# Latent attention in a four-layer kernel: score banks per head, a bank of its own for shared products, values in the first and third of four steps

## The chip, the cores and the metric

The kernel runs on one core of a Trainium2 chip. The metric is the device time of one execution in microseconds (us); lower is better. The engines are PE (TensorE; PEld is its weight load), DVE (VectorE), ACT (ScalarE), POOL (GpSimd) and SP (SyncE, which issues DMAs here).

## What is computed

The program runs a stack of layers on 2048 tokens of width 256: an expert layer, gated linear attention, the expert layer again, a dense expert layer, latent attention, and the dense expert layer again. Only latent attention is touched. Its reference, on a normalised input of 4 batches of 512 tokens with a residual added outside:

```python
q = (x @ W_q).reshape(B, S, 16, 128).transpose(0, 2, 1, 3)
latent = x @ W_kv_down                       # 64 wide
kv = (latent @ W_kv_up).reshape(B, S, 16, 128).transpose(0, 2, 1, 3)
scores = jnp.einsum('bhqd,bhkd->bhqk', q, kv) / sqrt(128)
probs = jax.nn.softmax(scores, axis=-1)
out = jnp.einsum('bhqk,bhkd->bhqd', probs, kv)
out = out.transpose(0, 2, 1, 3).reshape(B, S, 16 * 128)
return out @ W_o
```

The weights W_kv_up are folded into the queries (`absorb`) and into the output (`mix`) earlier in the program, so that every head works on the 64-wide latent.

## The kernel before

`latent_attention` works in steps. A step `s` is one tile of 128 query rows of one pair of heads; four steps (`TB`) make a pair, eight pairs (`PAIRS`) a batch, four batches the stage: 128 steps (`NS`) and 32 pairs (`NP`). The engines run their own programs over `s` and meet by semaphores. The order of the work is written out by hand in small tables.

One step goes through these parts, each named by the function that issues it:

- PE `scores(s)`: for each of two heads a product with the high and one with the low part of the latent (L2141, L2142), 128x512 each. Both heads go into one PSUM tile of two banks, `ps_s[s % 2]`, and `s_ready` counts once per step. It waits until the exponentials of step s-2 are done.
- DVE `row_max(s)` (L2381): one reduction over both heads, 1024 elements, gives the negated row maxima.
- ACT `exps(s)` (L2258): two exponentials, one per head, each with its row sum. Both wait for the one reduction.
- DVE `inverse(s)` (L2377): reciprocal of the two sums, when both exponentials are done.
- POOL (L2323): two products scale the probabilities, one per head.
- DVE `probs_turned` (L2388): a 32x32 block transposition of both heads' probabilities. It comes `TLAG` = 2 steps late, between `row_max` and `inverse`.
- PE `values(pair, half)` (L2159): the product of transposed probabilities and latent rows, in two halves of 64 blocks with 128 small matmuls, in two of four steps. It comes `VLAG` = 7 steps late, so that its halves fall on steps with s % 4 = 3 and s % 4 = 0. The result is in `ps_v`, four banks.
- ACT `oT_copy(pair)` (L2263): takes the values out of `ps_v`.

Beside these steps there are shared products, called `miscellany` in the code: queries of a later pair (L2120), a quarter or half of the output of the batch before (`mixed`, L2127), transpositions of the normalised input (L2095), the latent as columns (L2103) and as rows (L2110). They go into the first two banks of `ps_v`, in turn (`bank_of`), in the steps with s % 4 = 1 or 2 (`misc_at`); what stands where is said by `Q_AT`, `MIX_AT`, `TR_AT`, `LATT_AT`, `LATK_AT`. As the banks belong to the values too, `values(pair, 0)` waits until the last two shared products have been taken out of them:

```python
last = last_use(TB * pair + VLAG)
for n in (last - 1, last):
    evicted(pe, uses[n])
```

A product of queries is taken out by ACT in three copies, `q_high` (L2247 twice, L2251): the high parts of both heads, then the whole. POOL `q_low` (L2313, two operations back to back) makes the low parts. `RING` = 3 pairs of queries are kept. DVE's share beside the steps is the statistics and the normalisation of the next batch (L2337, L2341, L2347) and the evictions (L2353, L2361, L2370). SP spreads the latent rows over partitions with 16 DMAs per batch (L2303), which the first values of the batch wait for.

The whole PSUM, eight banks, is used: four by `ps_s`, four by `ps_v`.

## Time and profile before

| | |
|---|---|
| median of 3 runs | 1821.0 us (1817.26 to 1830.79) |
| the profiled execution | 1814.0 us, span 1812.3 us |
| PE busy | 82% of the span |
| DVE, ACT, POOL busy | 60%, 40%, 43% |
| latent attention, first score product to last step's | 1165.0 to 1647.1 us |

All durations are of the profiled execution, whose time is 1814.0 us. A matmul's row shows the time until its result is out, so that matmuls overlap; what PE needs for a piece of work is read from start to start.

### The profile page before, as it was taken

To read this page: it belongs to the slowest core of one execution; us is meant where nothing else is said; L and a number is where in the kernel's file an instruction comes from. 1 tells how busy PE (TensorE), PEld (TensorE's weight loads), DVE (VectorE), ACT (ScalarE), POOL (GpSimd) and SP (SyncE) were. 2 spreads that over 40 slices of the span, in tenths; PEclk is the share of its full clock that TensorE was granted. 3 is DMA by queue.
4 is the path that set the end of the run, shared out by engine and by line. 5 is a ranking of instruction groups with operands and counts; after the bars stand their busy time and mean duration, and the time that the engine had idled before them with its cause. 6 is when DMAs were issued, how large, how long until landed. Compare 5 with 4: busy or idle time off the path is not lost. (4 is left out here: it accounts for less than half of the span.)

```text
span 1812.3 us, 39345 instructions
## 1 busy us (share of the span) xinstructions
PE 1487.1 (82%) x14334; PEld 1022.4 (56%) x14334; DVE 1089.0 (60%) x2639; ACT 732.3 (40%) x1754; POOL 775.6 (43%) x741
## 2 busy tenths in 40 slices
PE   6888995758898978889993778778898887888798
PEld 3555563425555544555662656456576665666576
DVE  6852222476776547832224888576777676664788
ACT  5533332355555425533332111355545545443211
POOL 4453333753300004543336553286766766764000
PEclk9999998679999988899996888888999999989899
DMA  8319995321100005239972221000000000000000
GB/s 248 92 46 262 283 282 170 107 67 53 36 1 1 1 22 161 59 121 279 293 217 85 77 75 52 12 2 3 14 3 2 14 3 3 14 3 3 9 17 21
DMA packets 92662, 145.49 MB, mean 80 GB/s; under 512 B 25032, under 2 KB 52528, under 8 KB 92512
## 3 DMA queue, kind: packets, MB, share of 16 engines
q1 hardware_dynamic: 62816, 93.06, 17.8%
q0 software_dynamic: 15360, 37.77, 6.9%
q10 hardware_dynamic: 14336, 12.59, 2.5%
q8 instruction: 103, 1.69, 0.4%
q14 instruction: 47, 0.39, 0.1%
HBM read 122.39 MB, written 18.87 MB: 78 GB/s over the span
## 5 line engine op out<-in xcount | busy, mean ns | idle before, releaser
L2323 POOL TENSOR_TENSOR sb_m_prob<-sb_m_prob,sb_m_rinv 128x512 f32<-128x512 f32 x256 | 261.4, 1043 | 144.2 <-DVE sb_m_rinv L2377 141.8
L2258 ACT ACTIVATE sb_m_prob<-m_ps_s,sb_m_nmax 128x512 f32<-128x512 f32 x256 | 173.8, 684 | 231.8 <-DVE sb_m_nmax L2381 231.8
L1264 POOL DMA_INDIRECT sb_c_rows<-slot_rows,sb_slot x192 | 192.3, 1001 | 109.1 <-issue 52.0
L2159 PE MATMUL m_ps_v<-sb_m_pT,sb_m_lat_rows 32*64 32x128 f32 x8192 | 161.4, 301 | 61.5 <-ACT sb_m_q_whole L2251 36.2
L2381 DVE TENSOR_REDUCE sb_m_nmax<-m_ps_s 128x2 f32<-128x1024 f32 x128 | 155.8, 1217 | 90.4 <-PE m_ps_s L2142 89.6
L1098 POOL DMA_INDIRECT e_xn<-xn_rows,sb_table x128 | 118.3, 925 | 208.6 <-PE e_ps_x L1176 196.2
L1247 DVE TENSOR_TENSOR sb_e_h<-sb_e_sg,e_ps_gu 96x176 f32<-96x176 f32 x128 | 42.6, 333 | 255.6 <-ACT sb_e_sg L1223 255.6
L2159 PEld LDWEIGHTS m_ps_v<-sb_m_pT,sb_m_lat_rows 32*64 32x64 f32 x8192 | 140.7, 146 | 92.2 <-issue 82.2
L1185 PE MATMUL e_ps_gu<-e_wgu,sb_e_xT 128*96 128x352 f32 x512 | 176.4, 467 | 19.8 <-ACT sb_e_xT L1217 19.2
L2388 DVE STREAM_TRANSPOSE sb_m_pT<-sb_m_prob 128x1024 f32<-128x1024 f32 x128 | 158.0, 1234 | 1.0 <-POOL sb_m_prob L2323 1.0
L2141 PE MATMUL m_ps_s<-sb_m_latT_high,sb_m_qa 128*128 128x512 f32 x256 | 130.7, 511 | 16.5 <-ACT sb_m_prob L2258 13.7
L1202 PE MATMUL e_ps_y<-e_wdn,sb_e_hT 96*96 96x256 f32 x512 | 132.0, 381 | 0.0
L1278 DVE SCALAR_TENSOR_TENSOR sb_x<-sb_c_rows,sb_weight,sb_x 128x256 f32<-128x256 f32 (+1 forms) x192 | 92.5, 482 | 41.8 <-DMA sb_c_rows<-slot_rows,sb_slot 38.4
L1185 PEld LDWEIGHTS e_ps_gu<-e_wgu,sb_e_xT 128*96 128x96 f32 x512 | 73.6, 163 | 60.5 <-ACT sb_e_xT L1217 18.4
L702 PE MATMUL s_ps<-sb_r_xnT,sb_sguT 128*128 128x512 f32 (+1 forms) x192 | 102.2, 682 | 6.5 <-ACT sb_s_up L800 6.5
L2142 PE MATMUL m_ps_s<-sb_m_latT_low,sb_m_qa 128*128 128x512 f32 x256 | 106.4, 416 | 0.0
L293 PE MATMUL d_ps_e<-sb_d_we_high,sb_d_xT_high 128*128 128x512 f32 x256 | 98.7, 468 | 7.3 <-DVE sb_d_xT_low L414 7.3
L2313 POOL TENSOR_TENSOR sb_m_qa<-sb_m_q_whole,sb_m_qa 64x512 fp32r<-64x512 f32 x64 | 81.2, 1268 | 52.9 <-ACT sb_m_q_whole L2251 48.1
L1229 ACT ACTIVATE sb_e_y<-e_ps_y 96x256 f32<-96x256 f32 x128 | 48.7, 380 | 125.0 <-DMA slot_rows<-sb_e_y 91.5
L1775 POOL TENSOR_TENSOR sb_g_gw<-sb_g_g,sb_g_sig 128x512 f32<-128x512 f32 x8 | 11.6, 1448 | 201.2 <-ACT sb_g_sig L1687 201.2
L293 PE MATMUL d_ps_e<-sb_d_we_low,sb_d_xT_high 128*128 128x512 f32 x256 | 85.3, 416 | 0.0
L1217 ACT ACTIVATE sb_e_xT<-e_ps_x 128x192 f32<-128x192 f32 x128 | 42.1, 331 | 105.4 <-ACT sb_e_y L1229 50.2
(278 smaller groups left out, 3103.0 us busy)
## 6 DMA issues: line engine op xcount, KB each, us to landing
e_wgu<-wgu SPq DMA_DIRECT2D x128, 352.0 KB, 4.8
e_wdn<-wdn SPq DMA_DIRECT2D x128, 192.0 KB, 4.6
slot_rows<-sb_e_y ACTq DMA_DIRECT2D x128, 96.0 KB
xn_rows<-e_xn SPq DMA_DIRECT2D x16, 256.0 KB, 2.2
sb_c_rows<-slot_rows,sb_slot POOLq DMA_INDIRECT x192, 2.8
sb_x<-x SPq DMA_DIRECT2D x4, 512.0 KB, 5.6
e_xn<-xn_rows,sb_table POOLq DMA_INDIRECT x128, 5.0
sb_g_zm<-wqT SPq DMA_DIRECT2D x1, 2048.0 KB, 8.8
```

The costliest lines, as they stand in the source:

```text
L293: ins = pe.matmul(ps_e[j][:, :, :], xTs[u][xpart][:, c, :], we[wpart][:, c, 2 * j:2 * j + 2, :], start=(m == 0), stop=(m == 3 * DC - 1))
L1098: pool.indirect_dma_start(x, None, k.xn_rows[:, :], bass.IndirectOffsetOnAxis(ap=k.table[:, e:e + 1], axis=0))\
L1185: ins = pe.matmul(ps_gu[v][:, :], xT[v][:, c, :], wgu[(u - 1) % U][:, c, :], start=(c == 0), stop=(c == DC - 1))
L1202: ins = pe.matmul(ps_y[v][:, :], hT[v][:, c, :], wdn[(u - 3) % U][:, c, :], start=(c == 0), stop=(c == 1))
L1264: pool.indirect_dma_start(rows[u][j][:, :], None, k.slot_rows[:, :], bass.IndirectOffsetOnAxis(ap=k.slot[:, n, j:j + 1], axis=0))\
L2141: pe.matmul(to[:, hh, :], q[:, hh, cols], latT[b % 2][0][:, :], start=True, stop=False)
L2142: ins = pe.matmul(to[:, hh, :], q[:, hh, cols], latT[b % 2][1][:, :], start=False, stop=True)
L2159: ins = pe.matmul(ps_v[rows_of(hh), a, 0:P], lat_rows[b % 2][rows, kb // TB, kb % TB, :], of[rows, hh, :, kb, :], start=(kb == 0), stop=(k ...
L2258: act.activation(prob[s % 4][:, hh, :], ps_s[s % 2][:, hh, :], ACT.Exp, bias=nmax[s % 2][:, hh:hh + 1], accum_out=rsum[s % 2][:, hh:hh + 1 ...
L2323: pool.tensor_tensor(part, part, rinv[s % 2][:, hh:hh + 1].to_broadcast([P, T]), ALU.mult)\
L2381: dve.tensor_reduce(nmax[s % 2][:, :], ps_s[s % 2][:, :, :], AX, ALU.max, negate=True).then_inc(nmax_ready, 1)
L2388: dve.transpose(pT[pair % 2][:, :, t, :, :].rearrange("p h b i -> p h (b i)"), prob[s % 4][:, :, :]).then_inc(turned, 1)
```

## The change

Four things change, all of them in `latent_attention`; the arithmetic is the same.

- The scores have three banks, taken by head: product `j = 2 * s + hh` goes into `ps_s[j % 3]`, `s_ready` counts per head, `row_max` is two reductions of 512 elements, and each exponential waits for its own. `scores` waits head by head for the exponential three products back.
- The shared products have a bank for themselves, `bank`, used by one at a time; the values have `ps_v` alone, and their wait for evictions is gone. `mixed` fills 256 columns of it with one tile of 128 rows and is taken out at once, in the last batch partly by way of `ps_v`.
- The values come 8 steps late, their halves in steps with s % 4 = 0 and 2; queries in steps with s % 4 = 1, always of the pair after next; nearly all other shared products in steps with s % 4 = 3. The transposition of the probabilities is 3 steps late.
- ACT takes the whole query tile out of PSUM first, which frees the bank, and makes the high parts from that copy in SBUF. POOL's two low parts stand in two different steps.

```diff
-    TLAG, VLAG = 2, 7
+    TLAG, VLAG = 3, 8
-    Q_AT = {1: 2, 2: 3, 3: 4, 6: 5, 7: 6, 12: 7, 13: PAIRS, 15: PAIRS + 1}
-    MIX_AT = {4: (0, 0), 5: (0, 1), 8: (1, 0), 9: (1, 1)}
-    TR_AT = {10: 0, 11: 1}
-    LATT_AT, LATK_AT = 14, 0
+    TR_AT, MIX_AT = {18: 0, 22: 1}, {11: 0, 15: 1, 19: 2, 23: 3}
+    LATK_AT, LATT_AT = 3, 27
...
+        if e % TB == 1 and s // TB + 2 < NP:
+            return ("q", s // TB + 2)
...
-        ps_s = [ctx.enter_context(nc.psum_tensor(f"m_ps_s{u}", [P, 2, T], F32)) for u in range(2)]
+        ps_s = [ps(f"m_ps_s{u}", [P, T]) for u in range(3)]
         ps_v = ctx.enter_context(nc.psum_tensor("m_ps_v", [P, TB, T], F32))
+        bank = ps("m_bank", [P, 512])
...
             def take(key):
-                if use_at[key] >= 2:
-                    pe.wait_ge(bank_free[use_at[key] % 2], use_at[key] // 2)
-                return bank_of(key)
+                if use_at[key]:
+                    pe.wait_ge(bank_free, use_at[key])
...
-                if s >= 2:
-                    pe.wait_ge(p_ready, 2 * (s - 1))
                 cols = slice(t * P, (t + 1) * P)
                 for hh in range(2):
-                    pe.matmul(to[:, hh, :], q[:, hh, cols], latT[b % 2][0][:, :], start=True, stop=False)
-                    ins = pe.matmul(to[:, hh, :], q[:, hh, cols], latT[b % 2][1][:, :], start=False, stop=True)
-                ins.then_inc(s_ready, 1)
+                    j = 2 * s + hh
+                    if j >= 3:
+                        pe.wait_ge(p_ready, j - 2)
+                    pe.matmul(ps_s[j % 3][:, :], q[:, hh, cols], latT[b % 2][0][:, :], start=True, stop=False)
+                    pe.matmul(ps_s[j % 3][:, :], q[:, hh, cols], latT[b % 2][1][:, :], start=False, stop=True).then_inc(s_ready, 1)
...
-                    last = last_use(TB * pair + VLAG)
-                    for n in (last - 1, last):
-                        evicted(pe, uses[n])
...
-            for s in range(NS + VLAG - 2):
+            for s in range(NS + VLAG - 1):
                 if s < NS:
                     scores(s)
-                if s >= VLAG and (s - VLAG) % TB < 2:
-                    values((s - VLAG) // TB, (s - VLAG) % TB)
-                if misc_at(s) is not None:
-                    miscellany(misc_at(s))
+                if s >= VLAG and (s - VLAG) % TB in (0, 2):
+                    values((s - VLAG) // TB, (s - VLAG) % TB // 2)
+                if misc_of(s) is not None:
+                    miscellany(misc_of(s))
...
             def q_high(pair):
+                full(("q", pair))
                 if pair >= 2:
                     act.wait_ge(q_ready, 2 * (pair - 1))
-                act.activation(q_whole[pair % 2][:, :], bank_of(key), ACT.Copy).then_inc(bank_free[use_at[key] % 2], 1)
+                act.activation(q_whole[pair % 2][:, :], bank[:, :], ACT.Copy).then_inc(bank_free, 1)
+                if pair >= RING:
+                    act.wait_ge(s_ready, 2 * TB * (pair - RING + 1))
+                evicted(act, ("q", pair))
+                for hh in range(2):
+                    act.activation(qa[pair % RING][rows_of(hh), hh, :], q_whole[pair % 2][rows_of(hh), :], ACT.Copy)\
+                       .then_inc(high_ready, 1)
...
             def exps(s):
-                act.wait_ge(nmax_ready, s + 1)
                 for hh in range(2):
+                    j = 2 * s + hh
+                    act.wait_ge(nmax_ready, j + 1)
...
             def row_max(s):
-                dve.wait_ge(s_ready, s + 1)
-                dve.tensor_reduce(nmax[s % 2][:, :], ps_s[s % 2][:, :, :], AX, ALU.max, negate=True).then_inc(nmax_ready, 1)
+                for hh in range(2):
+                    j = 2 * s + hh
+                    dve.wait_ge(s_ready, j + 1)
+                    dve.tensor_reduce(nmax[s % 2][:, hh:hh + 1], ps_s[j % 3][:, :], AX, ALU.max, negate=True)\
+                       .then_inc(nmax_ready, 1)
```

On PE, in the middle of the first batch: `m_ps_s` are score products (four per step), `m_ps_v<-sb_m_pT` a half of the values (64 of one shape and 64 of another, shown as one row), `sb_absorb` the queries of a later pair. Before:

```order
L2159 MATMUL m_ps_v<-sb_m_pT,sb_m_lat_rows 64x128 x64
L2141 MATMUL m_ps_s<-sb_m_latT_high,sb_m_qa 128x512
L2142 MATMUL m_ps_s<-sb_m_latT_low,sb_m_qa 128x512
L2141 MATMUL m_ps_s<-sb_m_latT_high,sb_m_qa 128x512
L2142 MATMUL m_ps_s<-sb_m_latT_low,sb_m_qa 128x512
L2120 MATMUL m_ps_v<-sb_m_xT,sb_absorb 128x512 x2
L2141 MATMUL m_ps_s<-sb_m_latT_high,sb_m_qa 128x512
L2142 MATMUL m_ps_s<-sb_m_latT_low,sb_m_qa 128x512
L2141 MATMUL m_ps_s<-sb_m_latT_high,sb_m_qa 128x512
L2142 MATMUL m_ps_s<-sb_m_latT_low,sb_m_qa 128x512
L2120 MATMUL m_ps_v<-sb_m_xT,sb_absorb 128x512 x2
```

and with the change:

```order
L2137 MATMUL m_ps_v<-sb_m_pT,sb_m_lat_rows 64x128 x64
L2123 MATMUL m_ps_s<-sb_m_latT_high,sb_m_qa 128x512
L2124 MATMUL m_ps_s<-sb_m_latT_low,sb_m_qa 128x512
L2123 MATMUL m_ps_s<-sb_m_latT_high,sb_m_qa 128x512
L2124 MATMUL m_ps_s<-sb_m_latT_low,sb_m_qa 128x512
L2101 MATMUL m_bank<-sb_m_xT,sb_absorb 128x512 x2
L2123 MATMUL m_ps_s<-sb_m_latT_high,sb_m_qa 128x512
L2124 MATMUL m_ps_s<-sb_m_latT_low,sb_m_qa 128x512
L2123 MATMUL m_ps_s<-sb_m_latT_high,sb_m_qa 128x512
L2124 MATMUL m_ps_s<-sb_m_latT_low,sb_m_qa 128x512
L2137 MATMUL m_ps_v<-sb_m_pT,sb_m_lat_rows 64x128 x64
```

Before, a half of the values is followed by two products of queries in two successive steps, and the other half of the values stood right before; now queries and halves of the values alternate with one step's scores between all of them.

On DVE, early in the first batch (the digit is the buffer: `nmax` 0 or 1 by step, `ps_s` the score tile). Before:

```order
L2381 TENSOR_REDUCE sb_m_nmax0<-m_ps_s0 128x2
L2388 STREAM_TRANSPOSE sb_m_pT0<-sb_m_prob2 128x2x512
L2377 RECIPROCAL sb_m_rinv0<-sb_m_rsum0 128x2
L2381 TENSOR_REDUCE sb_m_nmax1<-m_ps_s1 128x2
L2388 STREAM_TRANSPOSE sb_m_pT0<-sb_m_prob3 128x2x512
L2377 RECIPROCAL sb_m_rinv1<-sb_m_rsum1 128x2
```

and with the change:

```order
L2338 TENSOR_REDUCE sb_m_nmax1<-m_ps_s1 128x1
L2338 TENSOR_REDUCE sb_m_nmax1<-m_ps_s2 128x1
L2346 STREAM_TRANSPOSE sb_m_pT0<-sb_m_prob2 128x2x512
L2332 RECIPROCAL sb_m_rinv1<-sb_m_rsum1 128x2
L2338 TENSOR_REDUCE sb_m_nmax0<-m_ps_s0 128x1
L2338 TENSOR_REDUCE sb_m_nmax0<-m_ps_s1 128x1
L2346 STREAM_TRANSPOSE sb_m_pT0<-sb_m_prob3 128x2x512
L2332 RECIPROCAL sb_m_rinv0<-sb_m_rsum0 128x2
```

Each step's reduction over two heads is split in two that read different banks, and the transposition works one step further back.

On POOL at the stage's start (`sb_m_qa` is a low part of queries, `sb_m_prob` a scaling). Before:

```order
L2313 TENSOR_TENSOR sb_m_qa<-sb_m_q_whole,sb_m_qa 64x512 x2
L2323 TENSOR_TENSOR sb_m_prob<-sb_m_prob,sb_m_rinv 128x512 x6
L2313 TENSOR_TENSOR sb_m_qa<-sb_m_q_whole,sb_m_qa 64x512 x2
L2323 TENSOR_TENSOR sb_m_prob<-sb_m_prob,sb_m_rinv 128x512 x2
L2313 TENSOR_TENSOR sb_m_qa<-sb_m_q_whole,sb_m_qa 64x512 x2
```

and with the change:

```order
L2271 TENSOR_TENSOR sb_m_qa<-sb_m_q_whole,sb_m_qa 64x512
L2282 TENSOR_TENSOR sb_m_prob<-sb_m_prob,sb_m_rinv 128x512 x2
L2271 TENSOR_TENSOR sb_m_qa<-sb_m_q_whole,sb_m_qa 64x512
L2282 TENSOR_TENSOR sb_m_prob<-sb_m_prob,sb_m_rinv 128x512 x6
L2271 TENSOR_TENSOR sb_m_qa<-sb_m_q_whole,sb_m_qa 64x512
```

The two low parts of a pair of heads stood together and now have the scalings of one step (two of them) between each other.

## Rows read from the trace of the kernel before

**Rows 1.** Groups of instructions by shape, stretch 1165 to 1665: busy us, mean ns, idle before.

```profile
L2323 POOL TENSOR_TENSOR sb_m_prob<-sb_m_prob,sb_m_rinv 128x512 f32<-128x512 f32 x256 | 261.4, 1043 | 144.2 <-DVE sb_m_rinv L2377 141.8
L2258 ACT ACTIVATE sb_m_prob<-m_ps_s,sb_m_nmax 128x512 f32<-128x512 f32 x256 | 173.8, 684 | 231.8 <-DVE sb_m_nmax L2381 231.8
...
L2381 DVE TENSOR_REDUCE sb_m_nmax<-m_ps_s 128x2 f32<-128x1024 f32 x128 | 155.8, 1217 | 90.4 <-PE m_ps_s L2142 89.6
...
L2313 POOL TENSOR_TENSOR sb_m_qa<-sb_m_q_whole,sb_m_qa 64x512 fp32r<-64x512 f32 x62 | 78.6, 1268 | 5.8 <-ACT sb_m_q_whole L2251 1.0
...
L2370 DVE TENSOR_TENSOR sb_x<-m_ps_v,sb_x 128x512 f32<-128x512 f32 x6 | 4.2, 692 | 3.3 <-PE m_ps_v L2127 3.3
...
L2361 DVE COPY sb_m_lat<-m_ps_v 128x256 f32<-128x256 f32 x3 | 1.3, 421 | 0.0
```

**Rows 2.** Waits in that stretch: engine and line waited for, us in total, times, longest.

```profile
DVE sb_m_nmax L2381 <- PE m_ps_s L2142: 89.6, 69, 5.4
...
DVE sb_m_rinv L2377 <- ACT sb_m_prob L2258: 52.3, 128, 1.5
PE m_ps_v L2159 <- ACT sb_m_q_whole L2251: 36.2, 16, 3.0
...
PE m_ps_v L2159 <- issue: 11.1, 14, 1.5
```

**Rows 3.** Timeline of DVE: start, us, instruction, idle before it.

```profile
1370.54 1.20 DVE L2381 TENSOR_REDUCE sb_m_nmax<-m_ps_s 128x2 f32<-128x1024 f32 x1
1371.66 1.24 DVE L2388 STREAM_TRANSPOSE sb_m_pT<-sb_m_prob 128x1024 f32<-128x1024 f32 x1
1373.26 0.17 DVE L2377 RECIPROCAL sb_m_rinv<-sb_m_rsum 128x2 f32<-128x2 f32 x1 [0.36 <-ACT sb_m_prob L2258]
1373.34 1.20 DVE L2381 TENSOR_REDUCE sb_m_nmax<-m_ps_s 128x2 f32<-128x1024 f32 x1
...
1378.53 1.23 DVE L2381 TENSOR_REDUCE sb_m_nmax<-m_ps_s 128x2 f32<-128x1024 f32 x1 [2.31 <-PE m_ps_s L2142]
```

**Rows 4.** Timeline of ACT in the same step.

```profile
1371.78 0.69 ACT L2258 ACTIVATE sb_m_prob<-m_ps_s,sb_m_nmax 128x512 f32<-128x512 f32 x1 [0.87 <-DVE sb_m_nmax L2381]
...
1372.46 0.68 ACT L2258 ACTIVATE sb_m_prob<-m_ps_s,sb_m_nmax 128x512 f32<-128x512 f32 x1
```

**Rows 5.** Timeline of PE: steps with shared products and values; last, values after a wait.

```profile
1326.01 3.62 PE L2127 MATMUL m_ps_v<-sb_mix,sb_m_oT 128*128 128x256 f32 x16
...
1330.50 2.08 PE L2159 MATMUL m_ps_v<-sb_m_pT,sb_m_lat_rows 32*64 32x128 f32 x128
...
1333.64 2.09 PE L2159 MATMUL m_ps_v<-sb_m_pT,sb_m_lat_rows 32*64 32x128 f32 x128
...
1336.99 1.98 PE L2120 MATMUL m_ps_v<-sb_m_xT,sb_absorb 128*128 128x512 f32 x4
...
1339.74 1.88 PE L2120 MATMUL m_ps_v<-sb_m_xT,sb_absorb 128*128 128x512 f32 x4
...
1373.86 3.51 PE L2159 MATMUL m_ps_v<-sb_m_pT,sb_m_lat_rows 32*64 32x128 f32 x128 [2.18 <-ACT sb_m_xT L2233]
```

**Rows 6.** Windows: busy us by engine, then the granted clock (PEclk), DMA share, GB/s.

```profile
1327.50:1340.00 12.50, 12.37 (x287) 9.15 (x286) 9.63 (x13) 6.83 (x19) 6.23 (x7) 1.00 0.01 3
...
1373.86:1375.50 1.64, 1.64 (x64) 1.64 (x70) 1.64 (x2) 0.92 (x3) 1.64 (x2) 0.50 0.00 0
...
1590.00:1602.50 12.50, 9.09 (x204) 6.45 (x203) 6.16 (x8) 5.83 (x15) 11.16 (x10) 0.73 0.01 3
```

**Rows 7.** Timeline of PE at the stage's start and at its last step.

```profile
1165.00 0.50 PE L2141 MATMUL m_ps_s<-sb_m_latT_high,sb_m_qa 128*128 128x512 f32 x1 [0.76 <-POOL sb_m_qa L2313]
...
1647.10 0.50 PE L2141 MATMUL m_ps_s<-sb_m_latT_high,sb_m_qa 128*128 128x512 f32 x1 [1.87 <-ACT sb_m_prob L2258]
```

**Rows 8.** The latent rows' tile: DMA issues on SP (ns), and their time to landing.

```profile
L2303 SPq DMA_DIRECT2D sb_m_lat_rows<-sb_m_lat x64: 585/601/1786, 1164.8 to 1555.1; - x64
...
DMA to landing us min/median/max: 1.9/1.9/3.3
```

More of the change, by code:

```diff
@@ L2026, in latent_attention @@
     uses = [("tr", 0, 0), ("tr", 0, 1), ("latT", 0), ("q", 0), ("q", 1), ("lat", 0)]
-    for d in range(NR):
-        if misc_of(d) is not None and misc_of(d) not in uses:
-            uses.append(misc_of(d))
-    uses += [("mix", B - 1, half) for half in range(2)]
+    uses += [misc_of(s) for s in range(NS) if misc_of(s) is not None]
+    uses += [("mix", B - 1, t) for t in range(2)]
     use_at = {key: n for n, key in enumerate(uses)}
@@ L2084, in take @@
             def take(key):
-                if use_at[key] >= 2:
-                    pe.wait_ge(bank_free[use_at[key] % 2], use_at[key] // 2)
-                return bank_of(key)
+                if use_at[key]:
+                    pe.wait_ge(bank_free, use_at[key])
             def transposed(b, half):
-                bank = take(("tr", b, half))
+                take(("tr", b, half))
                 for j in (2 * half, 2 * half + 1):
@@ L2098, in latent_columns @@
             def latent_columns(b):
-                bank = take(("latT", b))
-                evicted(pe, ("tr", b, 0))
+                take(("latT", b))
                 evicted(pe, ("tr", b, 1))
@@ L2106, in latent_rows @@
             def latent_rows(b):
-                bank = take(("lat", b))
+                take(("lat", b))
                 for j in range(TB):
@@ L2115, in queries @@
                 b, p = pair // PAIRS, pair % PAIRS
-                bank = take(("q", pair))
-                evicted(pe, ("tr", b, 0))
+                take(("q", pair))
                 evicted(pe, ("tr", b, 1))
@@ L2238, in latT_high @@
                 full(("latT", b))
-                act.activation(latT[b % 2][0][:, :], bank_of(("latT", b)), ACT.Copy).then_inc(high_ready, 1)
+                act.activation(latT[b % 2][0][:, :], bank[:, :], ACT.Copy).then_inc(high_ready, 1)
             def q_high(pair):
-                key = ("q", pair)
-                full(key)
-                if pair >= RING:
-                    act.wait_ge(s_ready, TB * (pair - RING + 1))
-                for hh in range(2):
-                    act.activation(qa[pair % RING][rows_of(hh), hh, :], bank_of(key)[rows_of(hh), :], ACT.Copy)\
-                       .then_inc(high_ready, 1)
+                full(("q", pair))
@@ L2281, in miscellany @@
                         latT_high(b + 1)
-                    if e == 5:
+                    if e == 10:
                         log_variance(b + 1)
-                    if e == 6:
+                    if e == 11:
                         inverse_deviation(b + 1)
-            for s in range(NS + VLAG + 1):
-                if s >= VLAG + 2 and (s - VLAG - 2) % TB == 0:
-                    oT_copy((s - VLAG - 2) // TB)
+            for s in range(NS + VLAG):
+                if s >= VLAG + 3 and (s - VLAG - 3) % TB == 0:
+                    oT_copy((s - VLAG - 3) // TB)
                 if s < NS:
                     exps(s)
-                if misc_at(s) is not None:
-                    miscellany(misc_at(s))
+                    miscellany(s)
         @block.sync
@@ L2428, in _ @@
                     inverse(s)
-                if d is not None:
-                    evictions(d)
-                    preparations(d)
-            for half in range(2):
-                add_out(B - 1, half)
+                    evictions(s)
+                    preparations(s)
+            add_out(B - 1, 0)
+            for t in range(2):
+                dve.wait_ge(v_ready, NP + t + 1)
+                x = k.X[:, B * TB - 2 + t, :]
+                dve.tensor_tensor(x, ps_v[:, t, 0:D], x, ALU.add)
+            add_out(B - 1, 1)
 def expert_layer(nc, k, r):
```

142 lines of the change are left out of this document (55 added, 87 removed).

## The prediction

> **What bounds the kernel now.** I read the page first: no engine is full over the whole span, so the touched stage has to be looked at by itself. It runs from the first score product at 1165.0 to the last step's at 1647.1 [rows 7], that is 482.1 us for 127 steps, 3.80 us a step or 15.2 us a pair of heads. Then I read the groups of instructions of this stretch for what each engine must do [rows 1], the waits for what it does not do [rows 2], and last the timelines of one pair, engine by engine, for the reason [rows 3 to 5].
>
> - DVE waits 89.6 us for scores and 52.3 us for exponentials [rows 2]. Without both it has 482 - 142 = 340 us of work, 10.6 us a pair.
> - POOL scales 8 times a pair at 1.043 and makes two low parts at 1.268 [rows 1]: 8.34 + 2.54 = 10.9, and with some gaps between them (estimated 0.3) 11.2 us.
> - ACT needs two exponentials a step, 0.68 from start to start [rows 4], which is 5.4 us a pair, and copies; it waits 231.8 us for DVE [rows 1]. It has room, but its copies can come at a bad moment.
> - PE I read from start to start at full clock [rows 5]. A step with half of the values: 1330.50 to 1333.64, 3.14. A step with queries: 1336.99 to 1339.74, 2.75. A step with a quarter of the output product: 1326.01 to 1330.50, 4.49; part of that is the start of the values, so 4.4. The half of the values itself is 2.08, so a step with scores alone is 3.14 - 2.08 = 1.06.
>
> So no engine is full, though three have 10.6 to 12 us of work for 15.2. The timelines show why. Two steps in a row DVE is bound by a chain through ACT: reduction at 1370.54, exponentials 1371.78 and 1372.46, reciprocal 1373.26 [rows 3, 4], next reduction at 1373.34 by the same spacing of 0.08: 2.80 us a step. Then DVE stands 2.31 us before the reduction at 1378.53, for scores [rows 3]. Those stand on PE behind the first half of the values, which began only at 1373.86, after 2.18 us of idle for an ACT eviction [rows 5]: the wait for the shared banks. It lets PE run ahead in the cheap steps and hold it in the dear ones. It also cools PE: the granted clock is 0.50, the lower level of 1.2 GHz, right after that idle, and 1.00 (2.4 GHz) in a stretch where PE is busy 12.37 of 12.50 us [rows 6]; that half of the values takes 3.51 instead of 2.08 [rows 5].
>
> **The change, part by part.**
>
> *Values without the wait.* PE's 36.2 us behind the query copies [rows 2] are only the named part; the other part is that DVE gets its scores late. In the new order halves of values and shared products alternate, one piece per step. PE's work a pair becomes 3.14 + 2.75 + 3.14 plus the fourth step: 1.06 with nothing, about 2.8 with latent rows or columns (priced like queries), 4.4 with output. That is 10.1, 11.8 and 13.4 us.
>
> *Three score banks, reductions by head.* The first exponential need not wait for the second reduction. A DVE operation on 512 elements of PSUM lasts 0.69, one on 256 0.42, the reduction of 1024 1.22 [rows 1]: about 0.53 per 512 elements and 0.15 fixed. From start to start the reduction takes 1.12 [rows 3], 0.06 fixed. With t = 0 at a step's first reduction: it lasts 0.69, the first exponential starts at 0.72 (0.04 later, as in rows 3 and 4), the second at 1.40, and the reciprocal 0.80 after that (1373.26 - 1372.46), at 2.20. DVE's own chain is two reductions at 0.59 from start to start, a transposition of 1.24 less the same overlap of 0.08, and the reciprocal's 0.08: 2.42. So DVE bounds this step, at 2.42 instead of 2.80. Splitting adds 0.06 to 0.15 a step: 128 times that is 8 to 19 us of DVE work, of which only what falls in pairs that PE does not bound counts. I take 0.06, since that is the spacing of rows 3. The Trainium skill (VectorE: DVE Perf Modes, "The TRN2 errata — SBUF-src ops pay a fixed extra latency per instruction") puts the measured fixed term at about 150 cycles for each DVE instruction. If it were paid in full 128 more times, the sum would be some 10 us worse; the duration in the rows agrees with it, the spacing is shorter.
>
> *Queries.* ACT's block after a query step is three copies of 512 elements, estimated at 0.6 each from the 0.68 of an exponential [rows 4], and a short wait for itself: 1.9, before about 1.8. It ends at 2.08 + 1.9 = 3.98, the next step's exponential wants 2.42 + 0.72 = 3.14; the reciprocal of that step comes about 0.7 late. Thus a pair that PE does not bound takes DVE's work, 10.6, 0.2 for the splits and 0.7 for this: 11.5, against POOL's 11.2. I take 11.7. Splitting the low parts in two steps removes no POOL work. It only keeps a scaling from being 2.5 us late.
>
> *One bank for all shared products.* Each must be taken out before the next is written. They are two steps apart, about 5 us, and an eviction takes one or two copies behind the exponentials, so this costs nothing in the stage. If it were not hidden, PE would stand one copy, 0.6 us, some 50 times: 30 us. Only in the prologue do they follow directly; there two transposed halves, columns and queries lose the overlap of copy and product: 2 to 4 us before the first score, I take 3.
>
> *Latent rows.* They move from step 1 to step 3 of a batch, the values that need them from 7 to 8. SP issues 16 DMAs at 0.6 and the last lands 1.9 later [rows 8]: 11.5 us. Between DVE's copy in step 3 and the values in step 8 lie five steps less PE's lead of about one, 12 us: 0 to 2 us for each of three batches, I take 1 in all.
>
> *Adding up.* First batch, no output product, PE light: 8 x 11.7 = 93.6. Second and third: 12.2 (rows) + 11.7 + four with output at 13.4, two of them with transpositions at +0.5 (54.7) + 12.1 (columns) + 11.7 = 102.4 each. Last: 12.2 + 11.7 + 53.7 + 10.3 + 10.3 (no more queries) = 98.2. Together 397 for 128 steps. From first to last score that is a step less, 394. To it come PE's gaps of issue, 11.1 us [rows 2], nearly all of which now lie on the path (10), and cold stretches that remain where PE has about 1 us of idle a pair (estimated 8). 394 + 10 + 8 = 412, against 482: 70 gained, less 3 in the prologue. The tail (last scaling, transposition, values, four output products) keeps its order: 0. The profiled execution of 1814 becomes 1747; the median of the runs shown, 1821, is 0.4% above it, so I forecast 1754.
>
> **The rivals.**
>
> *PE alone bounds, and runs without loss.* The cold stretches and gaps vanish, and pairs without output approach 11.2: 482 - 385 = 97, less 3, 1720, as a median 1727. For it: in the windows with output products PE is already full at clock 1.00 [rows 6]. Against it: PE is at most 1.5 steps ahead, since three banks hold three heads.
>
> *The chain through ACT stays the bound.* If semaphores and the query copies cost more than I allow, every step takes 3.3 us, the middle between 2.80 and 3.80, outside output steps: 116 x 3.3 + 12 x 4.4 = 436. Gain 46, less 3: 1771, as a median 1778. For it: DVE's one wait of 0.36 in each step [rows 3] is already of this kind.
>
> *The change does not do what it says.* The single bank and the tighter score ring wait as long as the old one: price 30 (above) plus PE waiting for exponentials in the steps without extra work, 0.7 in each of 48, 34: nearly all of 67, median about 1817. Against it: every shared product is two steps after the last.
>
> *Slower: the clock.* PE's work at full clock is 75 (first batch) + 98 + 98 + 91 = 362 us by the step prices. If many short idles in the new order hold the granted clock at the 0.73 of the poorest window [rows 6], this is 362 / 0.73 = 496, and with 10 of issue gaps 506 against 482: 24 + 3 slower, 1841, as a median 1848. It decides from 362 / 472 = 0.77 on. Against it: low clock in this trace stands behind idles of 2 us, which go. The Trainium skill (TensorE: Matmul & The Clock Gate, "A second HAM failure mode: psum-queue depth-cycling") tells of a kernel that cycled through PSUM banks and whose short idles made the clock oscillate; by that rule this rival would be the likely one. The trace speaks rather for long idles as the cause: no short one stands before the stretch at 0.50.
>
> **How the numbers follow.** Forecast (1754): 0.55. PE without loss (1727): 0.15. Chain through ACT (1778): 0.20. Change without its effect (1817): 0.05. Clock (1848): 0.05. The range reaches to the rivals on both sides, with the dear split and the unhidden copies in it: 1722 to 1798. About 1% is what a measurement of this kernel can tell from no change. Faster by over 1% (below 1803): 0.55 + 0.15 + 0.20 = 0.90; within 1%: 0.05; slower: 0.05.
>
> **What would show it.** In the profile of the changed kernel: the distance from the first score product to the last step's near 412 us; DVE's wait for scores down from 89.6 to under 40, and for exponentials from 52.3 to under 25; no wait of the values for a query copy; two reductions of 0.68 in each step, 2.4 to 2.5 us from step to step where PE is light; PE busy over 90% of the stage with granted clock above 0.95 in it. I would be wrong if PE stood for `bank` or for exponentials for more than 30 us, if the clock in the stage fell below 0.9, or if steps without output product took over 3.1 us while PE idles.

## The result and the profile after

The changed kernel takes 1748.6 us in the median of four runs (1736.8 to 1751.2), the kernel before, run beside it, 1825.9 (1817.3 to 1831.4): a ratio of 0.955 [0.951, 0.960]. Run again later, six executions gave a median of 1745.5 and a ratio of 0.956 [0.953, 0.959]. Forecast were 1754 us, in a range from 1722 to 1798.

The profiled execution took 1748.4 us, its span is 1746.6. Latent attention first, from its first score product to the last step's, on PE:

```profile
1186.60 0.48 PE L2123 MATMUL m_ps_s<-sb_m_latT_high,sb_m_qa 128*128 128x512 f32 x1
...
1583.28 0.50 PE L2123 MATMUL m_ps_s<-sb_m_latT_high,sb_m_qa 128*128 128x512 f32 x1
```

This is 396.7 us where [rows 7] gave 482.1. (Below, the distance is taken to the second head's product of that step, about 0.5 later: 482.7 before, 397.2 after.) Batch by batch, from one batch's first score product to the next one's, it is 90.6, 102.9, 104.2 and, for the last 31 steps, 99.0; before it was 116.9, 125.9, 128.1 and 111.2.

The stage gains 85 us and the span only 66. The stage's prologue, from its first transposition to its first score product, costs 2.7 us more (12.95 before, 15.63 now), and behind the last score product 1.9 us came back, 1.3 of them up to the start of the next layer. The other 19 were lost ahead of the stage, in code that the change doesn't touch: the first transposition starts at 1171.0 where it started at 1152.0. Some 14 us of this lie at one place, the copies of `absorb` on ACT, of which the last starts at 333.1 in the profile of before and here:

```profile
346.88 0.60 ACT L1713 ACTIVATE sb_absorb<-g_ps_at 128x512 f32<-128x512 f32 x1 [23.36 <-remote]
347.37 0.59 ACT L1713 ACTIVATE sb_absorb<-g_ps_o 128x512 f32<-128x512 f32 x1
```

In the profiles of the kernels below this copy starts anywhere from 338 to 353, whatever was edited. So a kernel's span in one profile is off by up to 20 us for a reason outside the stage, and the edits are judged by the stage's distance, and by medians where there are some. Some 12 of the 19 us fit the one profile of before: its execution, of 1814.0 us, is 12 under the median of 1825.9, while the changed kernel's, of 1748.4, is at its own. The medians differ by 77 us.

The groups of the stage after, as in [rows 1]: busy us, mean ns, idle before.

```profile
L2282 POOL TENSOR_TENSOR sb_m_prob<-sb_m_prob,sb_m_rinv 128x512 f32<-128x512 f32 x255 | 260.2, 1045 | 58.4 <-DVE sb_m_rinv L2332 53.9
L2219 ACT ACTIVATE sb_m_prob<-m_ps_s,sb_m_nmax 128x512 f32<-128x512 f32 x256 | 173.8, 683 | 132.6 <-DVE sb_m_nmax L2338 131.0
L2338 DVE TENSOR_REDUCE sb_m_nmax<-m_ps_s 128x1 f32<-128x512 f32 x256 | 164.1, 682 | 29.1 <-PE m_ps_s L2124 26.8
L2346 DVE STREAM_TRANSPOSE sb_m_pT<-sb_m_prob 128x1024 f32<-128x1024 f32 x126 | 155.3, 1233 | 0.0
```

Its waits, as in [rows 2]:

```profile
DVE sb_m_nmax L2338 <- PE m_ps_s L2124: 26.8, 43, 4.4
...
DVE sb_m_rinv L2332 <- ACT sb_m_prob L2219: 19.5, 31, 1.9
...
DVE sb_x L2326 <- PE m_bank L2108: 16.7, 12, 1.5
PE m_ps_s L2123 <- ACT sb_m_prob L2219: 16.3, 19, 1.9
...
PE m_ps_v L2137 <- issue: 4.1, 2, 2.3
```

The scalings, exponentials and transpositions last as long as before, and the two reductions of a step together 8 us in all longer than the one (164.1 against 155.8). What went are waits: DVE's for scores from 89.6 to 26.8, for exponentials from 52.3 to 19.5, ACT's for reductions from 231.8 to 131.0. The values' waits for shared products to be taken out, 36.2 us behind query copies and 6.6 behind copies of the transposed input before, are in no row. One wait has grown: DVE takes each output product out at once and waits for it, 16.7 us in the stage where it was 3.3. It falls in pairs that PE bounds. How full each engine is now, from the second batch's third pair on for 90 us, in a stretch with output products, at a batch's start, and over the whole stage (columns as in [rows 6]):

```profile
1310.00:1400.00 90.00, 89.33 (x2070) 67.64 (x2073) 76.22 (x129) 60.73 (x150) 75.28 (x71) 1.00 0.03 6
1322.50:1335.00 12.50, 12.50 (x290) 9.81 (x290) 10.47 (x20) 8.02 (x20) 9.97 (x10) 1.00 0.01 3
1400.00:1412.50 12.50, 9.28 (x245) 7.47 (x236) 7.92 (x17) 5.41 (x14) 10.46 (x10) 0.75 0.13 26
1186.60:1583.80 397.20, 372.80 (x8588) 275.89 (x8588) 330.49 (x560) 260.04 (x643) 334.79 (x314) 0.97 0.04 8
```

PE is busy for 94% of the stage at a granted clock of 0.97, and for 99% at 1.00 between two batch starts. In the stretch with output products, as in all 50 us from 1310 to 1360, it is busy all the time: there PE is the bound. A piece of DVE's timeline in the first batch shows what bounds a pair without output product:

```profile
1243.35 1.29 DVE L2338 TENSOR_REDUCE sb_m_nmax<-m_ps_s 128x1 f32<-128x512 f32 x2 [0.35 <-PE m_ps_s L2124]
1244.55 1.23 DVE L2346 STREAM_TRANSPOSE sb_m_pT<-sb_m_prob 128x1024 f32<-128x1024 f32 x1
1245.71 0.12 DVE L2332 RECIPROCAL sb_m_rinv<-sb_m_rsum 128x2 f32<-128x2 f32 x1
1245.76 1.26 DVE L2338 TENSOR_REDUCE sb_m_nmax<-m_ps_s 128x1 f32<-128x512 f32 x2
1246.94 1.23 DVE L2346 STREAM_TRANSPOSE sb_m_pT<-sb_m_prob 128x1024 f32<-128x1024 f32 x1
1248.10 0.12 DVE L2332 RECIPROCAL sb_m_rinv<-sb_m_rsum 128x2 f32<-128x2 f32 x1
```

From 1243.35 to 1245.76 is 2.41 us, and the reciprocal no longer waits: where [rows 3] had 0.36 us of idle before it in each step, DVE's own work is now nearly the whole step. (An `x2` stands for both heads' reductions; from the first to the transposition, 1245.76 to 1246.94, they take 1.18 us.)

### The profile page after: what moved, and what is told of

It is laid out like the page before. It is cut to its first block and busy times, and to the rows that moved or that the text cites. A ratio compares the mean times of both kernels' runs of the same rounds, so it can differ in the third digit from the quotient of the medians.

```text
span 1746.6 us, 39506 instructions
## 1 busy us (share of the span) xinstructions
PE 1448.2 (83%) x14334; PEld 997.1 (57%) x14334; DVE 1081.8 (62%) x2775; ACT 739.1 (42%) x1754; POOL 774.3 (44%) x741
## 5 line engine op out<-in xcount | busy, mean ns | idle before, releaser
L2219 ACT ACTIVATE sb_m_prob<-m_ps_s,sb_m_nmax 128x512 f32<-128x512 f32 x256 | 173.8, 683 | 132.6 <-DVE sb_m_nmax L2338 131.0
L2338 DVE TENSOR_REDUCE sb_m_nmax<-m_ps_s 128x1 f32<-128x512 f32 x256 | 164.1, 682 | 29.1 <-PE m_ps_s L2124 26.8
L2137 PE MATMUL m_ps_v<-sb_m_pT,sb_m_lat_rows 32*64 32x128 f32 x8192 | 139.1, 279 | 11.6 <-issue 8.1
L2137 PEld LDWEIGHTS m_ps_v<-sb_m_pT,sb_m_lat_rows 32*64 32x64 f32 x8192 | 123.0, 133 | 35.0 <-issue 31.3
L2123 PE MATMUL m_ps_s<-sb_m_latT_high,sb_m_qa 128*128 128x512 f32 x256 | 127.2, 497 | 16.4 <-ACT sb_m_prob L2219 16.3
L1185 PEld LDWEIGHTS e_ps_gu<-e_wgu,sb_e_xT 128*96 128x96 f32 x512 | 73.7, 163 | 58.4 <-ACT sb_e_xT L1217 13.7
L2124 PE MATMUL m_ps_s<-sb_m_latT_low,sb_m_qa 128*128 128x512 f32 x256 | 102.1, 399 | 1.2 <-issue 1.2
```

Of the source, the lines that this page charges most:

```text
L1185: ins = pe.matmul(ps_gu[v][:, :], xT[v][:, c, :], wgu[(u - 1) % U][:, c, :], start=(c == 0), stop=(c == DC - 1))
L2123: pe.matmul(ps_s[j % 3][:, :], q[:, hh, cols], latT[b % 2][0][:, :], start=True, stop=False)
L2124: pe.matmul(ps_s[j % 3][:, :], q[:, hh, cols], latT[b % 2][1][:, :], start=False, stop=True).then_inc(s_ready, 1)
L2137: ins = pe.matmul(ps_v[rows_of(hh), a, 0:P], lat_rows[b % 2][rows, kb // TB, kb % TB, :], of[rows, hh, :, kb, :], start=(kb == 0), stop=(k ...
L2219: act.activation(prob[s % 4][:, hh, :], ps_s[j % 3][:, :], ACT.Exp, bias=nmax[s % 2][:, hh:hh + 1], accum_out=rsum[s % 2][:, hh:hh + 1]).t ...
L2338: dve.tensor_reduce(nmax[s % 2][:, hh:hh + 1], ps_s[j % 3][:, :], AX, ALU.max, negate=True)\
```

## The experiments

The main theory is the prediction's: the gain has two parts, the split of reductions and exponentials by head, which breaks the chain through ACT, and shared products that no longer hold the values and the scores up. The rivals give one of the parts all of it, or put it down to the order alone. Line numbers are of each kernel itself. Distances are of the stage, as defined above, each from one profile; "one execution" stands where a kernel has no median.

| kernel | distance, us | ratio to before |
|---|---|---|
| before | 482.7 | |
| changed | 397.2, again 397.7 | 0.956 [0.953, 0.959] |
| before with the split alone | 451.9 | 0.987 [0.981, 0.994] |
| changed, halves adjacent | 468.0 | 0.994 [0.990, 0.998] |
| changed, halves adjacent, queries a step later | 427.7 | one execution |
| changed, eviction wait restored | 402.3 | 0.963 [0.956, 0.969] |
| changed, exponentials wait for both | 419.0 | one execution |
| changed, transposition two steps late | 398.7 | one execution |
| changed, latent rows earlier | 386.9 | 0.955 [0.948, 0.961] |
| changed, high parts from PSUM | 393.2 | one execution |
| both of the last two | 384.4 | 0.950 [0.946, 0.953] |
| both, and own banks at the start | 383.9 | 0.945 [0.942, 0.948] |

**The split alone, in the kernel before.**

```diff
-                dve.tensor_reduce(nmax[s % 2][:, :], ps_s[s % 2][:, :, :], AX, ALU.max, negate=True).then_inc(nmax_ready, 1)
+                for hh in range(2):
+                    dve.tensor_reduce(nmax[s % 2][:, hh:hh + 1], ps_s[s % 2][:, hh, :], AX, ALU.max, negate=True)\
+                       .then_inc(nmax_ready, 1)
...
-                act.wait_ge(nmax_ready, s + 1)
                 for hh in range(2):
+                    act.wait_ge(nmax_ready, 2 * s + hh + 1)
```

> The kernel before, with one part of the change alone: the reduction split by head and each exponential waiting for its own; banks, wait of the values and order as before. Measure: first score product to last step's, 482.1 us before and 397.0 with the change. Theory A (most of the gain is PE's work spread evenly and freed of the shared banks): only steps in which PE is not late gain their 0.38 us, so 462 to 478 us. Rival B (the shorter chain through ACT, 2.80 to 2.42 us a step, makes the gain): 128 x 0.38 = 49 us less, about 433.

The distance fell by 30.8 us to 451.9. The chain through ACT is broken as in the changed kernel, and what it leaves is made plain by its waits:

```profile
DVE sb_m_nmax L2382 <- PE m_ps_s L2142: 101.7, 76, 5.3
...
PE m_ps_v L2159 <- ACT sb_m_q_whole L2251: 28.7, 15, 2.4
...
DVE sb_m_rinv L2377 <- ACT sb_m_prob L2258: 9.7, 21, 0.9
```

DVE's wait for exponentials went from 52.3 to 9.7, and 12 of these 43 us came back as a longer wait for scores, 101.7 where there were 89.6. More than half of the change's gain is thus not in the split. Neither expectation came true: 451.9 is under theory A's range and well over rival B's 433.

**The changed kernel with both halves of the values in successive steps, as before.** Banks, split and lateness stay. One thing is not as before: the query product now stands in the step of the second half, where the old order had no shared product in a step with values.

```diff
-                if s >= VLAG and (s - VLAG) % TB in (0, 2):
-                    values((s - VLAG) // TB, (s - VLAG) % TB // 2)
+                if s >= VLAG and (s - VLAG) % TB in (0, 1):
+                    values((s - VLAG) // TB, (s - VLAG) % TB)
```

> The changed kernel, with the two halves of the values in steps with s % 4 = 0 and 1 instead of 0 and 2; banks, head by head waits and all else kept. Theory A: values, values, queries follow within two steps, 3.14 + 3.14 + 1.7 us of PE work against 2 x 2.42 of DVE's, 1 to 1.5 us late in each of 32 pairs: first to last score 425 to 445 us instead of 397.0. Rival B: order does not matter while the head by head chain stands, 392 to 402.

468.0 us, 71 more than the changed kernel and 16 more than the kernel before with the split alone; both expectations were too low. Of its waits three stand out:

```profile
DVE sb_m_nmax L2338 <- PE m_ps_s L2124: 101.2, 60, 2.9
...
ACT sb_m_q_whole L2205 <- PE m_bank L2101: 70.0, 31, 2.8
PE m_ps_s L2123 <- ACT sb_m_prob L2219: 56.7, 47, 1.9
```

The second of these rows stands in the changed kernel at 5.3 us, 3.5 of them in the prologue. Its cause is on ACT's timeline:

```profile
1341.86 0.68 ACT L2219 ACTIVATE sb_m_prob<-m_ps_s,sb_m_nmax 128x512 f32<-128x512 f32 x1
...
1344.98 0.60 ACT L2205 ACTIVATE sb_m_q_whole<-m_bank 128x512 f32<-128x512 f32 x1 [2.35 <-PE m_bank L2101]
1345.67 1.28 ACT L2210 ACTIVATE sb_m_qa<-sb_m_q_whole 64x512 fp32r<-64x512 f32 x2
1346.98 0.69 ACT L2219 ACTIVATE sb_m_prob<-m_ps_s,sb_m_nmax 128x512 f32<-128x512 f32 x1
```

The second half and the query product now share a step: PE gives the half 1340.94 to 1342.96 and starts the query product only then. ACT takes its instructions in order, so the copy of that product waits, and with it the exponentials of the next step.

**The same, with the queries one step later,** so that they don't share a step with values; the two transpositions of the input go where the queries were. Of all kernels here this one is nearest to the old order: two halves in a row, then two steps for shared products.

```diff
-    TR_AT, MIX_AT = {18: 0, 22: 1}, {11: 0, 15: 1, 19: 2, 23: 3}
+    TR_AT, MIX_AT = {17: 0, 21: 1}, {11: 0, 15: 1, 19: 2, 23: 3}
...
-        if e % TB == 1 and s // TB + 2 < NP:
+        if e % TB == 2 and s // TB + 2 < NP:
...
-                if s >= VLAG and (s - VLAG) % TB in (0, 2):
-                    values((s - VLAG) // TB, (s - VLAG) % TB // 2)
+                if s >= VLAG and (s - VLAG) % TB in (0, 1):
+                    values((s - VLAG) // TB, (s - VLAG) % TB)
...
```

> The changed kernel with the halves of the values in steps with s % 4 = 0 and 1, as in e3 (468.0 us from first to last score product, against 397.0), but with the queries in steps with s % 4 = 2 and the transpositions of the input in steps 17 and 21 of a batch. Theory D (e3 lost its 71 us because ACT, which takes the queries out in order, stood 66.5 us for a product that PE issues only after both halves, and its exponentials stood behind it): with the queries a step away the loss is mostly gone, 405 to 425 us. Rival E (two halves in successive steps starve DVE as such, 6.3 us of PE work for two steps of 2.4): 450 us or more.

427.7 us, just over theory D's range: of the 71 lost, 40 come back, and ACT's wait for the query product is 4.6 us again. The other 31 stay with two adjacent halves as such:

```profile
DVE sb_m_nmax L2338 <- PE m_ps_s L2124: 52.4, 70, 3.4
```

This kernel divides the gain. From the kernel before with the split alone to it are 24 us (451.9 to 427.7): what the new banks, the evictions that the values no longer wait for (28.7 us behind query copies with the split alone, none here), one query product per pair, the order of the query copies and the lateness give together while the halves stay adjacent. No run takes these apart, but for the lateness of the transposition, tried below. From it to the changed kernel are 31 us (427.7 to 397.2), for halves that stand apart. The 71 us that the first of the two variants lost overstate the order: 40 of them are a collision that the old order didn't have.

**The changed order with the values' wait for an eviction put back.**

```diff
+                    done = [use_at[misc_of(x)] for x in range(TB * pair + VLAG) if misc_of(x) is not None]
+                    evicted(pe, uses[max(done, default=5)])
```

> The changed kernel, with the wait put back alone: the first half of the values waits until the last shared product has been taken out of its bank (which they no longer share). Theory A: PE, up to 1.5 steps ahead, must let DVE or ACT catch up in each pair, 1 to 2 us in 31 pairs, partly with a cold PE after it: 430 to 460 us instead of 397.0. Rival B: under 5 us more.

402.3 us, 5 more; rival B had the size, and theory A's 430 to 460 failed. The values wait for a restored eviction in three places, 1.7 us in all, since a step of scores lies between the last shared product and the values; the other 3 us are not traced:

```profile
PE m_ps_v L2139 <- DVE sb_m_latT_low L2313: 1.7, 3, 0.6
```

So the wait is worth little in the new order. What it costs in the old one, where it stood behind 43 us of PE's idle, this run doesn't say; it is part of the 24 us above. The shared banks still stand behind the gain in another way: with them the values' own banks would have to be free for each shared product between two halves of one pair, whose sum is being formed there. That a kernel with shared banks can't have this order was argued from the code and not tried.

**Each exponential waits for both reductions.**

```diff
-                    act.wait_ge(nmax_ready, j + 1)
+                    act.wait_ge(nmax_ready, 2 * (s + 1))
```

> The changed kernel, but both exponentials of a step wait for both reductions. Split alone gained 30.8 us in the kernel before (451.9 against 482.7). Theory A: steps that PE does not bound (some 80 of 128) get 0.4 to 0.5 us longer, and PE gets its bank later: 415 to 430 us from first to last score instead of 397.0. Rival F (PE and POOL bound the new order anyway, the split no longer matters): under 403.

419.0 us, 21.8 more, as theory A had it. The wait before the reciprocal is back, 0.36 us as in [rows 3], and a light step of reductions, transposition and reciprocal is 2.86 us (1243.05 to 1245.91, where the next instruction starts):

```profile
1243.05 1.27 DVE L2338 TENSOR_REDUCE sb_m_nmax<-m_ps_s 128x1 f32<-128x512 f32 x2
1244.23 1.23 DVE L2346 STREAM_TRANSPOSE sb_m_pT<-sb_m_prob 128x1024 f32<-128x1024 f32 x1
1245.82 0.17 DVE L2332 RECIPROCAL sb_m_rinv<-sb_m_rsum 128x2 f32<-128x2 f32 x1 [0.36 <-ACT sb_m_prob L2219]
```

**The transposition of the probabilities two steps late instead of three** (`TLAG, VLAG = 2, 8`).

> The changed kernel, with the transposition of the probabilities two steps late instead of three (values still 8). Theory G: the third step of lag is needed in steps with a low part of queries on POOL (2.1 + 1.3 us of work, more than DVE's step), so DVE waits for POOL and stands before the reciprocal: 400 to 415 us instead of 397.0. Rival: PE's slack hides it, 396 to 399.

398.7 us, 1.5 more, in the rival's range and not in theory G's: no difference beyond what one profile can show (the changed kernel's two: 397.2, 397.7). The wait only changed its name: the transposition waits 25.7 us for the values' products to leave its buffer, and the waits for scores and exponentials shrink by as much.

```profile
DVE sb_m_pT L2346 <- PE m_ps_v L2137: 25.7, 23, 1.3
```

**The latent rows four steps earlier,** in the last step of the batch before.

```diff
-    LATK_AT, LATT_AT = 3, 27
+    LATK_AT, LATT_AT = 31, 27
...
-        if e == LATK_AT and b > 0:
-            return ("lat", b)
+        if e == LATK_AT and b + 1 < B:
+            return ("lat", b + 1)
...
```

> The changed kernel, with the latent rows of a batch made in the last step of the batch before (step 31 instead of 3), so that their 16 DMAs are done long before the first values. Theory C (the three batch starts with PE idle 1.8 to 2.3 us before the values, a cold half of 3.5 us and DVE idle 2.6 to 3.9 us are this DMA wait): 10 to 13 us less, 384 to 387. Rival: they are something else (instruction fetch, POOL's backlog), 0 to 3 us less.

386.9 us, 10.3 less, as theory C had it. In the changed kernel one batch starts like this on PE:

```profile
1404.03 0.50 PE L2123 MATMUL m_ps_s<-sb_m_latT_high,sb_m_qa 128*128 128x512 f32 x1 [0.92 <-ACT sb_m_prob L2219]
...
1407.05 3.72 PE L2137 MATMUL m_ps_v<-sb_m_pT,sb_m_lat_rows 32*64 32x128 f32 x128 [2.29 <-issue]
1410.70 0.80 PE L2123 MATMUL m_ps_s<-sb_m_latT_high,sb_m_qa 128*128 128x512 f32 x1
```

The idle of 2.29 us is called "issue", since the trace ties no releaser to it; what ends it is seen on SP, whose 16 DMAs are issued up to 1405.63. The last one lands at 1406.96, 0.09 us before the values start:

```profile
1393.73 11.90 SPq L2263 DMA_DIRECT2D sb_m_lat_rows<-sb_m_lat  x16
```

The same 0.09 us lie between the last landing and the values at the other two batch starts, 1304.06 to 1304.15 and 1511.30 to 1511.39. At the third, the trace names a transposition, which ends at that moment but is of the next pair:

```profile
1511.39 3.29 PE L2137 MATMUL m_ps_v<-sb_m_pT,sb_m_lat_rows 32*64 32x128 f32 x128 [2.63 <-DVE sb_m_pT L2346]
```

Behind the idle of 2.29 us the values take 3.72 us instead of 2.09, and DVE's next reduction waits 3.90. At the three batches the idle is 1.76, 2.29 and 2.63, the half of the values 3.48, 3.72 and 3.29, DVE's wait 2.64, 3.90 and 4.42, in all 10.96. With the rows earlier, DVE's longest wait for scores is 1.2 us and their sum 17.2 instead of 26.8. The median (1740.0) gained 5.5 and not 10 us against the changed kernel's 1745.5. What fits is that in this kernel's profile the prologue took 21.2 us and ran wholly at a granted clock of 0.50, where the changed kernel's took 15.6 at 0.79 in both of its profiles; whether the other executions were so too, no profile tells.

**The high parts of the queries from PSUM first, the whole last,** as in the kernel before.

```diff
...
-                act.activation(q_whole[pair % 2][:, :], bank[:, :], ACT.Copy).then_inc(bank_free, 1)
...
-                    act.activation(qa[pair % RING][rows_of(hh), hh, :], q_whole[pair % 2][rows_of(hh), :], ACT.Copy)\
+                    act.activation(qa[pair % RING][rows_of(hh), hh, :], bank[rows_of(hh), :], ACT.Copy)\
                        .then_inc(high_ready, 1)
+                act.activation(q_whole[pair % 2][:, :], bank[:, :], ACT.Copy).then_inc(bank_free, 1)
...
```

> The changed kernel, with ACT's three query copies in the old order: the high parts from PSUM first, then the whole, which frees the bank 1.2 us later; POOL waits for the whole. Theory: the bank is wanted two steps later, so nothing on the path changes; a copy from PSUM is 0.59 against 0.63 us from SBUF, without the wait in between: 393 to 398 us instead of 397.0. Rival H (the single bank is tight): 403 or more.

393.2 us, within the theory's range and 4.0 less in the stage, but 4.9 more in the prologue (20.5), where two query products and the latent rows follow one another in the one bank. The second query product and the rows each wait for all three copies of the product before, 1.92 us instead of 0.69, and then take 2.82 and 3.68 us instead of 1.98 and 2.00; the prologue's granted clock is 0.67 in the mean where it was 0.79.

**Both of these together.**

> The changed kernel with both alterations that shortened it: latent rows in the last step of the batch before (e1, 386.9 us) and the high parts of the queries from PSUM (e4, 393.2 us). If their gains of 10.3 and 4.0 us add, 383 us from first to last score product and some 12 to 14 us less in all than the changed kernel; if both only fill the same gaps, 386 to 388.

384.4 us: the two gains add but for 1.6 us. The median is 1735.4, 10.1 under the 1745.5 of the changed kernel, where 12 to 14 were expected.

**And the prologue's products in the four banks of `ps_v`,** which no values use yet; the second query product alone goes into `bank`.

```diff
+    first = [("latT", 0), ("lat", 0)]
+    uses = [("tr", 0, 0), ("tr", 0, 1), ("q", 0), ("q", 1)]
...
+        early = {("tr", 0, 0): 0, ("tr", 0, 1): 1, ("latT", 0): 2, ("lat", 0): 0, ("q", 0): 3}
+
+        def bank_of(key):
+            return ps_v[:, early[key], :] if key in early else bank
...
-                if use_at[key]:
+                if key not in first and use_at[key] >= 4:
                     pe.wait_ge(bank_free, use_at[key])
...
```

> c1, with the five products before the first scores in banks of ps_v (still empty then) and one in the shared bank, so that none waits for the eviction of the one before. Before the change the prologue from first transposition to first score took 13.0 us, with it 15.6 (21.2 and 20.5 in two runs at low granted clock). Theory: the waits for evictions are the loss, 11 to 13 us; the rest as c1, so 3 to 5 us less in all. Rival: at the clock's lower level the products themselves take the time, and nothing is gained.

```profile
1160.26 1.94 PE L2092 MATMUL m_ps_v<-sb_ident,sb_m_xn 128*128 128x128 f32 x8 [6.01 <-DVE sb_m_xn L2323]
1162.88 3.78 PE L2099 MATMUL m_ps_v<-sb_m_xT,sb_wkv 128*128 128x512 f32 x4 [0.69 <-ACT sb_m_xT L2209]
1166.46 2.82 PE L2115 MATMUL m_ps_v<-sb_m_xT,sb_absorb 128*128 128x512 f32 x4
1169.12 1.88 PE L2115 MATMUL m_bank<-sb_m_xT,sb_absorb 128*128 128x512 f32 x4
1170.83 1.89 PE L2106 MATMUL m_ps_v<-sb_wkv,sb_m_xT 128*128 128x64 f32 x16
1173.95 0.50 PE L2137 MATMUL m_ps_s<-sb_m_latT_high,sb_m_qa 128*128 128x512 f32 x1 [1.23 <-POOL sb_m_qa L2288]
```

The prologue is 13.7 us, with two waits of 0.69 and 1.23 left in it, where the changed kernel, in its second profile, has five that sum to 4.3. The median is 1725.1 (1722.4 to 1730.0), 20 us under the changed kernel and 99 under the 1824.5 of the kernel before: the best of all. Against the kernel with both alterations it gained 10.3 us where 3 to 5 were expected: that kernel's prologue had taken 20.5 us in its profile, so 6.8 of them are there and 0.5 in the stage, and the rest is not accounted for.

## Why the prediction was right

The time was forecast 5 us too high, the distance 15 (412 against 397). That the time is nearer than the distance is in part luck: the forecast starts from a median of 1821.0, and the kernel before, run beside the changed one, had 1825.9. The gain was forecast as 67 us and measured as 77.

- **The split.** Predicted: 2.80 us a step becomes 2.42, at 0.06 us for the split. Measured: 2.41, with 1.18 us for two reductions from start to start, the 0.59 each that the prediction took. With the joint wait put back it is 2.86. The Trainium skill (VectorE: DVE Perf Modes, "The TRN2 errata — SBUF-src ops pay a fixed extra latency per instruction") gives a fixed term of about 150 cycles for each DVE instruction. A reduction's 682 ns agrees with that as a duration, but back to back the second costs 0.06 us more than its elements, so the 10 us that this rule would have added did not come.
- **Pairs without output product.** Predicted 11.7 us each, eight of them 93.6; the first batch took 90.6. One pair (1239.88 to 1251.00) is 11.1. The cause is as predicted, DVE's own work in such steps.
- **Pairs with output product.** Predicted 13.4 us, bound by PE, at full clock. The window from 1310.00 has PE busy 89.33 of 90.00 us at 1.00, and from one output product to the next are 13.3 to 13.7 us. The second and third batch were to take 102.4 each and took 102.9 and 104.2; the last, 98.2 less a light step, 95.6, and took 99.0. The latent rows' loss is in all three: without it they take 100.8, 99.7 and 93.5.
- **Two terms on top, 18 us, were too much.** Added were 10 us of issue gaps and 8 of cold clock to the 394 of the steps' sum. The distance is 396.7 in all, with 10.3 of a loss in it that the sum had at 1. The steps were priced from start to start and a little high (a light pair at 11.7), which already covered such gaps, and the idles of 0.69 us once a pair left the granted clock at 1.00 in the windows between batch starts.
- **Latent rows: the step that failed.** "0 to 2 us for each of three batches, I take 1 in all." It is 10.3. The wait itself came out near the top of the foreseen range or above it, 1.8 to 2.6 us each time, as the 16 DMAs took 13.2 to 13.6 us from the first issue to the last landing and not 11.5: they are issued 0.75 us apart where [rows 8] has 0.6. What the term left out altogether is what follows from it, a half of the values of 3.3 to 3.7 us at the lower clock and DVE without scores for 2.6 to 4.4 us. The prediction had the very pattern in [rows 5], 3.51 us after 2.18 of idle, and used it for the kernel before only.
- **Values without the wait: right in sum, open in name.** The heading gave to one cause what are two at least. Of the 55 us that remain of the gain after the split's 31, 24 come with adjacent halves still, by the banks, the wait and what goes with them, and 31 only when the halves stand apart. Putting the wait back in the new order costs 5. Why halves apart are worth 31 us was argued and not tried; the reading that fits: by the ring of three banks PE can't be more than 1.5 steps ahead, so a step in which it has two pieces of about 2 us is paid by DVE, and one in which it has none can't make up for it.
- **Query copies.** Predicted: the next reciprocal 0.7 late. Measured 0.52 to 0.58 a pair.
- **Prologue.** Predicted 3 us, measured 2.7. **Tail.** Predicted 0, measured 1.3 less up to the next layer.
- **The rivals.** PE alone without loss gave 385 us, and the kernel with the rows earlier has 386.9. That is its number and not its mechanism: in a light pair DVE bounds the step, at 2.41 us, and PE does not. The chain through ACT did not hold (19.5 us of waits). PE stood for exponentials for 16.3 us, under the 30 that would have spoken for a change without effect. The clock is 0.97 in the stage, and the rival that a ring of banks with short idles would lower it fell. The Trainium skill (TensorE: Matmul & The Clock Gate, "A second HAM failure mode: psum-queue depth-cycling") tells of a kernel that cycled through PSUM banks and whose short idles made the clock go down and up. That is not seen here, since low clock stands in the changed kernel's stage only behind idles of 1.8 to 2.6 us (window 1400.00 to 1412.50, at 0.75 in the mean). With adjacent halves, though, the clock in the stage is 0.92, and it is 0.50 from 1244.98 to 1251.81 behind an idle of 1.48 us. So the rival fell by the idles that this order leaves, not by the ring of banks as such.

## What to carry to other kernels

Where engines meet through a short ring of buffers, deal out the large pieces of the leading engine one per step: here two of them in neighbouring steps cost 31 us of the stage, and a third in the step of the second cost 40 more, since an in-order engine that takes out a late piece holds up everything queued behind it. A rare wait of 2 us is to be priced with what it sets off, the slower clock after it and the follower's idle: three of them cost 10 us here. And where steps are priced from start to start, gaps of issue need no term of their own. Before a variant is called "the old order", look for what the old order didn't have: the first one here had such a collision in it, and made the order seem worth 71 us.

## What the runs showed of the hardware

- ACT's copy of 64x512 elements takes 629 ns from SBUF and 588 ns from PSUM. The change reads the high parts from SBUF, 64 copies, which is 2.6 us of ACT's time; how much of the 4 us that taking them from PSUM gave is due to this was not separated.
- The prologue's granted clock differs between kernels whose prologue is the same code: 0.79 over 15.6 us in the changed kernel, in both of its profiles, and 0.50 over 21.2 us with the latent rows earlier. What makes the difference was not settled.
- The copies of `absorb` end between 333 and 353 us in thirteen profiles, in code that is the same in all: at 333.7 in the profile of before, and from 339 on in the others.
- DVE's normalisation of 128x256 elements is shorter in the stage of the changed kernel (the second row) than in the one before (the first), by 4.3 us of busy time:

```profile
L2347 DVE TENSOR_SCALAR sb_m_xn<-sb_x,sb_m_mv,sb_m_rstd 128x256 f32<-128x256 f32 x12 | 10.2, 888 | 0.0
...
L2306 DVE TENSOR_SCALAR sb_m_xn<-sb_x,sb_m_mv,sb_m_rstd 128x256 f32<-128x256 f32 x12 | 5.9, 495 | 0.0
```

The traces tell what goes with it. Of the 208 in thirteen profiles, 134 had POOL at work during less than 0.8 of their time, and took 382 to 416 ns; the 74 with POOL at work during more took 414 to 1422 ns. So such an instruction lasts up to over three times as long beside POOL's products. No edit moved POOL's work alone.
